# Reordering the opening of a fused cross-attention kernel: form casts and norm statistics later, first loads signalled one by one

## The chip, the cores and the metric

One Trainium2 chip, one core of it. The metric is the device time of one execution in microseconds (us). The engines are TensorE (PE; PEld is its weight load), VectorE (DVE), ScalarE (ACT), GpSimd (POOL) and SyncE (SP), which issues nearly all DMA transfers. Everything is float32; the large products are made of three passes over a rounded part and a remainder of each operand.

## The reference, cut to what matters

First a small attention without softmax over each of 8 batch entries, then two cross-attentions with layer norms and an MLP. Shapes: `x` and the context are (8, 256, 512).

```python
# layer 0, per batch entry b (x_2 is the context)
g_x     = (g_w @ x_2 + g_b).T          # (512, 128)
theta_x = (theta_w @ x + theta_b).T    # (512, 128)
phi_x   = phi_w @ x_2 + phi_b          # (128, 512)
y  = ((theta_x @ phi_x) / 512 @ g_x).T
x  = bn_gamma * (w_w @ y + w_b - bn_mean) * rsqrt(bn_var + eps) + bn_beta + x
# layer 1, seen as (4, 512) tokens a tile group; kv_in is the context both times
h  = layer_norm(x)
x  = x + softmax((h @ wq + bq) @ (ctx @ wk + bk).T / sqrt(128)) @ (ctx @ wv + bv) @ wo + bo   # twice
x  = x + gelu(layer_norm(x) @ w_fc1 + b_fc1) @ w_fc2 + b_fc2
```

## The kernel before, in words

The kernel has a front and a main part. The front computes all keys and values from the context and stores them in DRAM (`kd`, `vd`); the main part walks over heads and token chunks. The change touches the front alone.

The front goes twice over half of the batch: `p` = 0 (batch entries 0 to 3) and `p` = 1 (entries 4 to 7). Each half starts with an **opening** and goes on with eight **rounds** (`r` = 0 to 7, then 8 to 15). `front_order()` writes the order of all units of work out by hand; TensorE, ScalarE and VectorE each walk the same list and do their share of each unit, so the list is the program order of all three. GpSimd and SP have loops of their own.

The opening of a half, in the list written by `opening(p)`, has these units:

- `pg` (two per entry, L1029): the context times the weights of phi and g. VectorE adds the bias and writes `pg` (L1341).
- `M` (L1036): phi and g are multiplied to a 128x128 matrix. ScalarE copies it to `msb` (L1085).
- `th` (L1033): theta from `x`, needs the transfer of `xb`. ScalarE adds the bias and writes `th` (L1083).
- `WM` (L1038): `msb` times the output weights. ScalarE copies it to `wm` (L1087).
- `wy` (two, L1040): `wm` times `th`. ScalarE scales and shifts into `aff` (L1096), VectorE adds `xb` and writes a tile of `x` (L1346). In the kernel before VectorE then takes this tile's statistics for the first layer norm (`tile_stats`, L1312), and after each fourth tile their aggregate and one small addition (`moments`, L1318 and L1320).
- `B` (four blocks `B11, B12, B22, B21` for each of `i` = 0, 1): the context is transposed into a bank of `U` (L876). ScalarE writes the rounded part (`plain`, L1104) and a copy of B12 (`us`, L1108); VectorE writes the remainders (L1362) and four sums and differences, the **forms** T1 to T4 (`temp`, L1371, L1375, L1380, L1385). ScalarE casts each form (`tform`, L1111), and GpSimd makes the form's remainder (`forms_lo`, L647). The forms and their remainders are first needed by the round's products (L842 to L844).

The units `pg`, `M`, `th`, `WM` and `wy` take turns on four PSUM banks (`S` twice, `T`, `O`, by `l0_bank`), so each waits for the reading of the fourth unit before it. The `B` blocks and the units of the rounds take turns on the four banks of `U` (`take`); the second four `B` blocks therefore wait until VectorE is done with the first four.

After the `wy` units of the second entry of a half, ScalarE casts the seven forms of the first key weights (`key_cast`, L1122); GpSimd makes their remainders (`key_form`, L668). A round has 14 key products (`K`, about 1.36 us each on TensorE), and then 14 value products (`V`, in two quarters `q` of seven). VectorE sums these up (`products`, `values`). For the next round VectorE makes three sums of value weights (`value_sums`, L1436, L1439, L1441), in round 0 and 8 right after the opening.

SP issues the loads in its own order: the first context chunk (four loads into `x` that share the semaphore `ctx_in_c[0]`), the weights `wpg` and the bias `pgb_s` (both on `l0_w`), the next chunk, `wth` and `www_s`, `xb` for entry 0, key weights and so on. Each context tile lies in `x`, which is later overwritten by the result. `load_x(b)` for `b` > 1 waits for the counter `z_x` (tiles of `x` written), and behind `load_x(2)` stand the context chunks 2 and 3 and the first value weights.

The wait with which the first product begins, and the place of the form casts in ScalarE's program, are:

```python
pe.wait_ge(ctx_in_c[b // 2], 64)
if name == ("pg", 0, 0):
    pe.wait_ge(l0_w, 32)
...
for form in {B11: (), B12: (T1,), B22: (T3, T2), B21: (T4,)}[blk]:
    act.wait_ge(formed, base + FORMED_BY[p][form])
    act.activation(tform[p][:, 0, form, i, :], temp(i, form), ACT.Copy).then_inc(t_hi, 1)
```

Of the kernel before, what the change touches and what calls it, by code (L numbers as in the profile page):

```python
# [38 lines left out]
P = 128  # L39
# [46 lines left out]


B11, B12, B22, B21 = range(4)
T1, T2, T3, T4 = range(4)
# [40 lines left out]
def opening(p):  # L130

    def blocks(i):
        return [("B", p, i, blk) for blk in range(4)]

    b = 4 * p
    out = [("pg", b, 0), ("pg", b, 1)] + blocks(0)
    for b in range(4 * p, 4 * p + 4):
        more = b + 1 < 4 * p + 4
        out += [("M", b, 0)] + ([("pg", b + 1, 0)] if more else [])
        out += [("th", b, 0), ("WM", b, 0)] + ([("pg", b + 1, 1)] if more else [])  # L140
        out += blocks(1) if b == 4 * p else []
        out += [("wy", b, 0), ("wy", b, 1)]
    return out

# [119 lines left out]
def bass_xattn(nc, x_in, ctx_in, thw, thb, pgw, pgb, www, bncol, wa, wk, wv, wb, hcol, vrow,  # L264
               lncol, f1col, orow, out):
    ctx = ExitStack()
    with ctx:
# [100 lines left out]
        ctx_in_c, x_in_b, l0_w = [sem(f"ctx_in_{c}") for c in range(CHUNKS)], [sem(f"x_in_b{i}") for i in range(2)], sem("l0_w")  # L368
        l0_w2 = sem("l0_w2")
        ident_zero, ident_ready = sem("ident_zero"), sem("ident_ready")  # L370
# [99 lines left out]
        def _(sp):  # L470
# [62 lines left out]

            load_chunk(0)
            sp.dma_start(wpg[:], pgw).then_inc(l0_w, 16)
            sp.dma_start(pgb_s[:], pgb.partition_broadcast(P)).then_inc(l0_w, 16)
            load_chunk(1)
# [88 lines left out]
        def _(pool):  # L626
# [146 lines left out]
            for r in range(ROUNDS):  # L773
# [18 lines left out]
                if not end:  # L792
# [4 lines left out]
                    for k in range(5 if r + 1 < ROUNDS - 1 else 0):  # L797
                        value_form(r + 1, k)
                if r == GROUPS:
                    for c in range(CHUNKS):  # L800
                        deviation(0, c)
# [37 lines left out]
        def _(pe):  # L839
# [33 lines left out]
            def turned_context(o, c, ch):  # L873
                pe.wait_ge(ctx_in_c[c], 64)
                for t in range(4):
                    mm = pe.transpose(o[:, t * P:t * P + P], x[:, 4 * c + t, ch * P:ch * P + P], ident[:])  # L876
                return mm
# [125 lines left out]
            def first_attention(what, b, part):  # L1003
                name = (what, b, part)
                if what == "pg":
                    pe.wait_ge(ctx_in_c[b // 2], 64)
                    if name == ("pg", 0, 0):
                        pe.wait_ge(l0_w, 32)
                elif what == "th":
                    pe.wait_ge(l0_w2, 32)  # L1010
                    pe.wait_ge(x_in_b[b % 2], 16 * (b // 2 + 1))
                elif what == "M":
                    pe.wait_ge(z_free_v, l0_taken(("pg", b, 1), TO_V))
                elif what == "WM":
                    pe.wait_ge(z_free_a, l0_taken(("M", b, 0), TO_A))
                elif what == "wy" and part == 0:
                    pe.wait_ge(z_free_a, l0_taken(("WM", b, 0), TO_A))
# [52 lines left out]
        def _(act):  # L1070
# [28 lines left out]
            def blocks(p, i, blk):  # L1099
                base = formed_before(p, i)  # L1100
                act.wait_ge(unit, UNIT["B", p, i, blk] + 1)
# [3 lines left out]
                if blk == B12:  # L1105
                    if p and i == 0:
                        act.wait_ge(summed, sums_before(GROUPS))
                    act.activation(middle(i), bank("B", p, i, blk), ACT.Copy).then_inc(copied, 1)  # L1108
                for form in {B11: (), B12: (T1,), B22: (T3, T2), B21: (T4,)}[blk]:
                    act.wait_ge(formed, base + FORMED_BY[p][form])  # L1110
                    act.activation(tform[p][:, 0, form, i, :], temp(i, form), ACT.Copy).then_inc(t_hi, 1)  # L1111
# [128 lines left out]
            for what, *a in FRONT:  # L1240
# [12 lines left out]
                elif what == "q":  # L1253
                    if a[2] == 1:
                        queries(*a[:2])
                elif what == "L":
                    exponentials(0)
                elif what == "X":
                    divided(0)
                elif what in TO_A:  # L1260
                    first_attention(what, *a)
                    if what == "wy" and a[0] % 4 == 1 and a[1] == 1:
                        for k in range(7):
                            key_cast(GROUPS * (a[0] // 4), 0, k)

# [29 lines left out]
        def _(dve):  # L1295
# [18 lines left out]
            def moments(n, c):  # L1314
# [5 lines left out]
                dve.tensor_scalar(vpe[:, 4 * c:4 * c + 4], mv[:, 4 * c:4 * c + 4, 1], EPS, None, ALU.add).then_inc(ln_eps, 1)  # L1320

            def normalise(n, c, own=range(4)):

# [10 lines left out]
            def first_attention(what, b, part):  # L1334
                name = (what, b, part)
                o = l0_bank(*name)
                if what == "pg":
                    if b == 4 and part == 0:
                        dve.wait_ge(v_form, 7 * GROUPS)
                    dve.wait_ge(z_unit, L0[name] + 1)  # L1340
                    dve.tensor_tensor(pg[:, 2 * part:2 * part + 2, :], o.rearrange("p (a n) -> p a n", a=2),  # L1341
                                      pgb_s[:].unsqueeze(1).to_broadcast([P, 2, 256]), ALU.add).then_inc(z_free_v, 1)
                elif what == "wy":
                    k = 2 * b + part
                    dve.wait_ge(z_free_a, l0_taken(name, TO_A))
                    dve.tensor_tensor(x[:, k, :], aff[:, part, :], xb[:, b % 2, part, :], ALU.add).then_inc(z_x, 1)  # L1346
                    dve.wait_ge(z_x, k + 1)
                    tile_stats(k)
                    if k % 4 == 3:
                        moments(0, b // 2)  # L1350

# [187 lines left out]
            for k, (what, *a) in enumerate(FRONT):  # L1539
# [10 lines left out]
                elif what == "V":  # L1550
                    r, q, product_of = a
                    values(*a)
                    if (r + 1) % GROUPS and r + 1 < ROUNDS - 1 and q == 0 and product_of in (P6, P7, P3):
                        value_sums(r + 1, (P6, P7, P3).index(product_of))
# [130 lines left out]
```

## Time and profile before

| what | us |
|---|---|
| median of 3 runs (2339.66 to 2346.64) | 2343.88 |
| the profiled execution | 2339.65 |
| its span | 2337.8 |
| PE busy in the span | 2281.9 (98%) |
| DVE, ACT, POOL busy | 1411.3, 1165.5, 1250.0 |
| first opening on TensorE | 9.70 to 59.96 |
| second opening on TensorE | 375.51 to 420.60 |

The profiled execution has 1.85 us outside its span. In the rows of the profile "idle before <-releaser" gives how long the engine had been idle before an instruction and what ended this. TensorE's granted clock is given as a share of its full 2.4 GHz; 0.50 is its lower level, 1.2 GHz. A timeline row with xN is N instructions in a row; its second number is from the first one's start to the last one's end, and TensorE's products overlap their neighbours by some 0.15 us, so that differences of starts are better durations.

### The profile page before, as it was taken

How to read it: one execution, taken by the hardware profiler on the slowest of the kernel's cores; microseconds unless marked ns; L12 is line 12 of the kernel's file. 1: busy time of each engine (PE TensorE's matmuls, PEld its weight loads, DVE VectorE, ACT ScalarE, POOL GpSimd, SP SyncE). 2: the span in 40 equal slices, each digit the busy share in tenths (PEclk: the TensorE clock that was granted, in tenths of full speed). 3: DMA queues.
4: the chain of work that ended last, by engine and by line, in shares of the span. 5: the costliest groups of instructions: out<-in, count | busy, mean ns of one | idle time of the engine just before them, and what ended most of it. 6: DMA issues, size and time to landing. Idle time of an engine off the chain costs nothing.

```text
span 2337.8 us, 36326 instructions
## 1 busy us (share of the span) xinstructions
PE 2281.9 (98%) x13192; PEld 1989.4 (85%) x13192; DVE 1411.3 (60%) x2380; ACT 1165.5 (50%) x2967; POOL 1250.0 (53%) x983
## 2 busy tenths in 40 slices
PE   7999998999999999999999989999999998999999
PEld 5899997899997888888888878888888887788887
DVE  4666666666665666666666776666666666534433
ACT  3323232322224766666666767666666666422222
POOL 3877772887757674344443775644435545611110
PEclk9999999999999999999999999999999999999999
DMA  4454543354544222222222212222222220100001
GB/s 170 145 190 163 190 163 118 127 198 156 194 159 137 72 73 73 69 73 73 66 79 65 73 55 64 73 78 64 76 70 80 75 64 19 36 28 28 27 1 72
DMA packets 83439, 218.33 MB, mean 93 GB/s; under 512 B 9536, under 2 KB 12096, under 8 KB 83264
## 3 DMA queue, kind: packets, MB, share of 16 engines
q1 hardware_dynamic: 82544, 215.91, 27.5%
q8 instruction: 108, 1.77, 0.3%
q14 instruction: 67, 0.55, 0.1%
q10 hardware_dynamic: 720, 0.10, 0.0%
HBM read 144.41 MB, written 71.57 MB: 92 GB/s over the span
## 4 chain that ended last, share of the span: by engine, by line
PE 87%; ACT 5%; DVE 4%; POOL 1%; issue 1%; DMA 1%; SPq 0%; DVEq 0%; ACTq 0%
PE U L842 22%; PE U L844 22%; PE U L843 22%; PE T L987 4%; PE O L842 2%; PE S L844 2%; PE O L844 2%; PE O L843 2%; PE S L843 2%; PE S L842 2%; DVE hT L1494 1%; ACT probs L1221 1%; ACT aff L1180 1%; PE S L1029 1%; ACT probs L1213 1%
## 5 line engine op out<-in xcount | busy, mean ns | idle before, releaser
L1513 DVE TENSOR_TENSOR x<-x,U 128x512 f32<-128x512 f32 x384 | 261.1, 683 | 80.8 <-PE U L844 78.5
L1213 ACT ACTIVATE probs<-S,nm 128x257 f32<-128x257 f32 x512 | 238.2, 477 | 35.8 <-DVE nm L1521 35.8
L1521 DVE TENSOR_REDUCE nm<-S 128x2 f32<-128x514 f32 x256 | 177.3, 692 | 123.1 <-PE S L844 119.3
L1231 ACT ACTIVATE PT<-T 128x512 fp32r<-128x512 f32 x256 | 152.6, 596 | 173.4 <-PE T L987 172.4
L1221 ACT ACTIVATE probs<-probs,rs 128x256 f32<-128x256 f32 x512 | 230.0, 499 | 0.5 <-DVE rs L1525 0.5
L842 PE MATMUL U<-wos,oT 128*128 128x512 f32 x512 | 213.5, 417 | 0.2 <-DVE gT L1504 0.2
L1536 DVE SCALAR_TENSOR_TENSOR oT<-O,hc,oT 128x256 fp32r<-128x256 f32 x256 | 123.8, 484 | 144.0 <-ACT oT L1237 144.0
L739 POOL CAST vb<-vb 128x1024 fp32r<-128x1024 f32 x64 | 68.0, 1063 | 262.4 <-DMA vb<-vd 262.4
L844 PE MATMUL U<-wos,oT 128*128 128x512 f32 x512 | 202.0, 395 | 0.0
L843 PE MATMUL U<-wos,oT 128*128 128x512 f32 x512 | 201.2, 393 | 0.0
L1529 DVE TENSOR_TENSOR PT<-T,PT 128x512 fp32r<-128x512 f32 x256 | 175.5, 686 | 42.0 <-ACT PT L1231 42.0
L1237 ACT ACTIVATE oT<-O,hc 128x256 fp32r<-128x256 f32 x256 | 121.3, 474 | 126.7 <-PE O L844 126.7
L987 PE MATMUL T<-ident,probs 128*128 128x128 f32 x1024 | 154.8, 273 | 14.4 <-ACT probs L1221 14.2
L1199 ACT ACTIVATE tmp<-U,f1c 128x512 f32<-128x512 f32 x64 | 44.0, 688 | 246.1 <-PE U L844 246.1
L733 POOL TENSOR_TENSOR kb<-kb 128x1032 fp32r<-128x1032 f32 x64 | 156.1, 2439 | 5.2
L1504 DVE TENSOR_TENSOR gT<-tmp,gT 128x512 fp32r<-128x512 f32 x64 | 57.2, 893 | 165.8 <-ACT gT L1207 165.8
L842 PE MATMUL U<-hT,wqs 128*128 128x512 f32 x384 | 155.6, 405 | 1.0 <-DVE hT L1494 1.0
L741 POOL TENSOR_TENSOR vb<-vb 128x1024 fp32r<-128x1024 f32 x64 | 153.7, 2402 | 5.1
L842 PE MATMUL S<-kb,qT 128*128 128x258 f32 x512 | 146.5, 286 | 7.2 <-ACT probs L1213 7.2
L844 PE MATMUL U<-hT,wqs 128*128 128x512 f32 x384 | 150.7, 392 | 0.0
L843 PE MATMUL U<-hT,wqs 128*128 128x512 f32 x384 | 150.0, 391 | 0.0
L844 PE MATMUL S<-kb,qT 128*128 128x258 f32 x512 | 145.1, 283 | 0.0
(246 smaller groups left out, 7242.3 us busy)
## 6 DMA issues: line engine op xcount, KB each, us to landing
kd<-stage SPq DMA_DIRECT2D x128, 258.0 KB, 2.5
kb<-kd SPq DMA_DIRECT2D x64, 516.0 KB, 3.4
vd<-stage SPq DMA_DIRECT2D x128, 256.0 KB, 2.1
vb<-vd SPq DMA_DIRECT2D x64, 512.0 KB, 3.8
raw<-wk SPq DMA_DIRECT2D x32, 512.0 KB, 5.3
rawv<-wv SPq DMA_DIRECT2D x28, 512.0 KB, 4.5
raw<-wa SPq DMA_DIRECT2D x24, 512.0 KB, 4.6
raw<-wb SPq DMA_DIRECT2D x24, 512.0 KB, 5.0
```

Of the source, the lines that this page charges most:

```text
L733: pool.tensor_tensor(lo_part_of, f(lo_part_of), f(hi_part_of), ALU.subtract).then_inc(k_lo, 1)
L741: pool.tensor_tensor(lo_part_of, f(lo_part_of), f(hi_part_of), ALU.subtract).then_inc(v_lo, 1)
L842: pe.matmul(o, lhs[0], rhs[0], start=start, stop=False)
L843: pe.matmul(o, lhs[0], rhs[1], start=False, stop=False)
L844: return pe.matmul(o, lhs[1], rhs[0], start=False, stop=stop)
L987: mm = pe.transpose(T[:, at_:at_ + P], probs[:, J % 2, qt, tt * P:tt * P + P], ident[:])
L1213: ins = act.activation(probs[:, r, qt, 0:257], S[:, qt, 0:257], ACT.Exp, bias=nm[:, r, qt:qt + 1], scale=-1.0, accum_out=sums[:, r, qt:qt ...
L1221: ins = act.activation(probs[:, r, qt, 0:256], probs[:, r, qt, 0:256], ACT.Copy, scale=rs[:, r, qt:qt + 1])
L1231: act.activation(PT[:, J % 2, 0, :], T[:], ACT.Copy).then_inc(pt_hi, 1)
L1513: dve.tensor_tensor(x[:, tile, :], x[:, tile, :], bank(what, s, t), ALU.add).then_inc(free, 1)
L1521: dve.tensor_reduce(nm[:, J % 2, :], S[:, :, 0:257], AX.X, ALU.min).then_inc(least, 1)
L1529: dve.tensor_tensor(PT[:, J % 2, 1, :], T[:], f(PT[:, J % 2, 0, :]), ALU.subtract).then_inc(pt, 1)
```

## The change

- In `opening`, the order of the units is another. For the first entry: `M`, `th`, the second four `B` blocks, `WM`, `pg` of the next entry, the two `wy`, the next entry's second `pg`. For the other entries `th` now stands in front of `pg` of the next entry.
- ScalarE's casts of the forms (L1111) leave `blocks` and stand in new units `t`: one behind all units of the half's first entry, one behind those of the second, there with the seven key casts behind it, which keep their place.
- VectorE's `tile_stats` and `moments` leave the opening. Eight tiles' statistics of a half are taken beside the first eight value products of the half's second round (rounds 1 and 9). GpSimd's four `deviation` operations go from the end of its round 8 to that of round 10.
- SP loads `wpg` first; the first context chunk comes as two loads of two tiles each, with a semaphore each (`ctx_first`, `ctx_in_c[0]`); the bias `pgb_s` follows with its own semaphore (`l0_b`), for which VectorE waits in place of TensorE.

```diff
 def opening(p):
-    b = 4 * p
-    out = [("pg", b, 0), ("pg", b, 1)] + blocks(0)
-    for b in range(4 * p, 4 * p + 4):
-        more = b + 1 < 4 * p + 4
-        out += [("M", b, 0)] + ([("pg", b + 1, 0)] if more else [])
-        out += [("th", b, 0), ("WM", b, 0)] + ([("pg", b + 1, 1)] if more else [])
-        out += blocks(1) if b == 4 * p else []
+    first = 4 * p
+    out = [("pg", first, 0), ("pg", first, 1)] + blocks(0)
+    for b in range(first, first + 4):
+        early, more = b == first, b + 1 < first + 4
+        out += [("M", b, 0), ("th", b, 0)]
+        out += blocks(1) if early else [("pg", b + 1, 0)] if more else []
+        out += [("WM", b, 0)]
+        out += [("pg", b + 1, 0)] if early else [("pg", b + 1, 1)] if more else []
         out += [("wy", b, 0), ("wy", b, 1)]
+        out += [("pg", b + 1, 1)] if early else []
+        out += [("t", p, b - first)] if b < first + 2 else []
     return out
...
-            load_chunk(0)
             sp.dma_start(wpg[:], pgw).then_inc(l0_w, 16)
-            sp.dma_start(pgb_s[:], pgb.partition_broadcast(P)).then_inc(l0_w, 16)
+            for i, arrived in enumerate((ctx_first, ctx_in_c[0])):
+                sp.dma_start(x[:, 2 * i:2 * i + 2, :], ctx_in[0, 2 * i:2 * i + 2].rearrange("t p n -> p t n")).then_inc(arrived, 16)
+            sp.dma_start(pgb_s[:], pgb.partition_broadcast(P)).then_inc(l0_b, 16)
             load_chunk(1)
...
-                if r == GROUPS:
+                if r == GROUPS + 2:
                     for c in range(CHUNKS):
                         deviation(0, c)
...
 # scalar engine
-                for form in {B11: (), B12: (T1,), B22: (T3, T2), B21: (T4,)}[blk]:
-                    act.wait_ge(formed, base + FORMED_BY[p][form])
+            def forms(p, i):
+                for form in T_ORDER:
+                    act.wait_ge(formed, formed_before(p, i) + FORMED_BY[p][form])
                     act.activation(tform[p][:, 0, form, i, :], temp(i, form), ACT.Copy).then_inc(t_hi, 1)
...
-                    if what == "wy" and a[0] % 4 == 1 and a[1] == 1:
-                        for k in range(7):
-                            key_cast(GROUPS * (a[0] // 4), 0, k)
+                elif what == "t":
+                    forms(*a)
+                    for k in range(7 if a[1] else 0):
+                        key_cast(GROUPS * a[0], 0, k)
...
 # vector engine
+            def first_norm(p, n):
+                if n < TILES // 2:
+                    dve.wait_ge(z_x, TILES // 2 * (p + 1))
+                    tile_stats(TILES // 2 * p + n)
+                    if n % 4 == 3:
+                        moments(0, 2 * p + n // 4)
...
-                    dve.wait_ge(z_x, k + 1)
-                    tile_stats(k)
-                    if k % 4 == 3:
-                        moments(0, b // 2)
...
                     values(*a)
+                    if r % GROUPS == 1:
+                        first_norm(r // GROUPS, 7 * q + product_of)
```

TensorE's waits follow the loads: entry 0 and the first-chunk blocks wait for `ctx_first`, entry 1 and the blocks for `ctx_in_c[0]` too, and the first product for `wpg` alone.

## Rows read from the trace of the kernel before

**Rows 1.** Waits of TensorE over the span: us in total, times, longest us.
```profile
PE S L1029 <- DMA pgb_s<-pgb: 9.7, 1, 9.7
...
PE S L1038 <- ACT msb L1085: 5.7, 2, 3.0
PE O L1033 <- ACT aff L1096: 5.6, 2, 3.3
PE U L842 <- DVE us L1412: 2.3, 2, 1.1
PE S L1033 <- issue: 1.5, 1, 1.5
...
PE U L842 <- POOL wks L668: 0.4, 2, 0.2
```

**Rows 2.** Timeline of TensorE, first opening: start us, us, instructions, idle before.
```profile
9.70 6.22 PE L1029 MATMUL S<-wpg,x 128*128 128x256 f32 x16 [9.70 <-DMA pgb_s<-pgb]
15.76 1.91 PE L876 MATMUL U<-ident,x 128*128 128x128 f32 x16
...
44.80 1.05 PE L1036 MATMUL S<-pg 128*128 128x128 f32 x8
45.69 1.89 PE L1029 MATMUL S<-wpg,x 128*128 128x256 f32 x8
47.42 1.88 PE L1033 MATMUL T<-xb,wth 128*128 128x512 f32 x4
49.13 0.59 PE L1038 MATMUL O<-www_s,msb 128*128 128x256 f32 x2
...
53.01 1.05 PE L1036 MATMUL O<-pg 128*128 128x128 f32 x8
```

**Rows 3.** Windows: stretch, length, busy us (instructions) by engine, granted clock, DMA share, GB/s.
```profile
22.00:25.00 3.00, 0.01 (x1) 0.00 (x0) 2.36 (x5) 2.19 (x6) 2.63 (x3) 1.00 0.00 0
25.00:28.40 3.40, 3.39 (x8) 2.73 (x9) 0.33 (x1) 0.92 (x2) 1.14 (x1) 0.51 0.00 0
...
35.30:37.40 2.10, 0.00 (x0) 0.00 (x0) 1.34 (x3) 1.40 (x3) 2.08 (x3) 1.00 0.00 0
...
388.00:394.60 6.60, 6.60 (x39) 5.33 (x40) 2.35 (x5) 3.55 (x7) 1.70 (x2) 1.00 0.00 0
```

**Rows 4.** Timeline of ScalarE, first opening.
```profile
24.16 0.63 ACT L1111 ACTIVATE tform<-temp 128x512 fp32r<-128x512 f32 x1 [0.81 <-DVE temp L1385]
...
45.68 0.41 ACT L1122 ACTIVATE wks<-raw 128x256 fp32r<-128x256 f32 x1
...
47.82 0.26 ACT L1085 ACTIVATE msb<-S 128x128 f32<-128x128 f32 x1
```

**Rows 5.** Timeline of VectorE, first opening and the start of round 0.
```profile
18.97 0.69 DVE L1371 TENSOR_TENSOR temp<-us,U 128x512 f32<-128x512 f32 x1 [2.33 <-ACT us L1108]
...
24.05 0.68 DVE L1362 TENSOR_TENSOR plain<-U,plain 128x512 fp32r<-128x512 f32 x1
24.65 0.68 DVE L1341 TENSOR_TENSOR pg<-O,pgb_s 128x512 f32<-128x512 f32 x1
...
63.75 1.15 DVE L1436 TENSOR_TENSOR v_s<-early_v 128x512 f32<-128x512 f32 x1
```

**Rows 6.** Timeline of GpSimd, start of round 0.
```profile
63.60 0.75 POOL L668 TENSOR_TENSOR wks<-raw,wks 128x256 fp32r<-128x256 f32 x1 [8.95 <-ACT wks L1122]
```

**Rows 7.** Timeline of VectorE, value products of round 1.
```profile
126.71 0.69 DVE L1478 TENSOR_TENSOR vt<-vt,U 128x512 f32<-128x512 f32 x1 [0.75 <-PE U L844]
...
132.84 0.69 DVE L1470 TENSOR_TENSOR vt<-U,vb 128x512 f32<-128x512 f32 x1
```

**Rows 8.** DMA issues from 0.7 to 0.75 and from 3.0 to 3.1 us: size, us to landing.
```profile
x<-ctx_in SPq DMA_DIRECT2D x1, 256.0 KB, 3.5
...
wpg<-pgw SPq DMA_DIRECT2D x1, 256.0 KB, 5.1
pgb_s<-pgb SPq DMA_DIRECT2D x1, 128.0 KB, 6.5
```

More of the change, by code:

```diff
@@ L368, in bass_xattn @@
         ctx_in_c, x_in_b, l0_w = [sem(f"ctx_in_{c}") for c in range(CHUNKS)], [sem(f"x_in_b{i}") for i in range(2)], sem("l0_w")
-        l0_w2 = sem("l0_w2")
+        l0_w2, l0_b, ctx_first = sem("l0_w2"), sem("l0_b"), sem("ctx_first")
         ident_zero, ident_ready = sem("ident_zero"), sem("ident_ready")
@@ L873, in turned_context @@
             def turned_context(o, c, ch):
-                pe.wait_ge(ctx_in_c[c], 64)
+                if c == 0:
+                    pe.wait_ge(ctx_first, 16)
+                pe.wait_ge(ctx_in_c[c], 64 if c else 16)
                 for t in range(4):
@@ L1005, in first_attention @@
                 if what == "pg":
-                    pe.wait_ge(ctx_in_c[b // 2], 64)
+                    if b < 2:
+                        pe.wait_ge(ctx_first, 16)
+                    if b:
+                        pe.wait_ge(ctx_in_c[b // 2], 64 if b > 1 else 16)
                     if name == ("pg", 0, 0):
-                        pe.wait_ge(l0_w, 32)
+                        pe.wait_ge(l0_w, 16)
                 elif what == "th":
@@ L1099, in blocks @@
             def blocks(p, i, blk):
-                base = formed_before(p, i)
                 act.wait_ge(unit, UNIT["B", p, i, blk] + 1)
@@ L1339, in first_attention @@
                         dve.wait_ge(v_form, 7 * GROUPS)
+                    if b == 0 and part == 0:
+                        dve.wait_ge(l0_b, 16)
                     dve.wait_ge(z_unit, L0[name] + 1)
```

## The prediction

> **What bounds the kernel now.** I read the page first: TensorE is busy for 98% of the span, so only its idle or slow time can be won. Then its waits, over the whole span [rows 1]: the longest is the 9.7 us before its first product, put down to `pgb_s`, and four more lie in the two openings: `WM` on `msb` (3.0 and 2.7), the second entry's `th` on `aff` (3.3 and 2.2), `th` of entry 3 on what the profile calls issue (1.5, its `xb` transfer), and in rounds 0 and 8 the sixth product on VectorE's `us` (1.1 and 1.2), with 0.4 on GpSimd's key remainders. The rest of the waits lie in the main part, which the change leaves alone. Third, the windows on either side of the stalls, for the granted clock [rows 3]: a stall of 3.0 us (22 to 25) is followed by 3.4 us at 0.51, the lower level (1.2 GHz); one of 2.1 us (35.3 to 37.4) is followed by the same, at 38.8 to 42.1, and the 3.3 us stall of the second opening too, at 400.6 to 403.9; the 2.7 us stall is not (1.00 behind it). (Of these three falls the first has its rows; the others look the same.) So three of four stalls cost 3.4/2 = 1.7 us of slow products on top. Last the timelines of the other engines, for why these waits exist.
>
> **Why they exist.** In the first four `B` blocks VectorE and ScalarE hand work to each other: ScalarE's cast of a form waits for VectorE (0.81 idle, [rows 4]), and the next block's `plain` stands behind that cast, for which VectorE's next form waits. `msb` and `th` stand behind all of it. VectorE takes from 18.97 to 24.65 for seven operations [rows 5], each 0.60 from start to start (24.05 to 24.65), so 4.2 us of work in 5.7. The second four blocks do the same to `aff`, on which the bank of the next `th` hangs.
>
> **The change, part by part.** All times come from differences of starts of the undisturbed third entry [rows 2]: `M` 0.89, a `pg` 1.73, `th` 1.71, then `WM`, `pg` and two `wy` together 3.88 (0.43 + 1.73 + 1.72); an entry is 8.2. Four `B` blocks take 1.74 (15.76 to 17.50), 0.44 each.
>
> *First loads.* TensorE began at 9.70 because `l0_w` counted `pgb_s` too, which landed at 3.05 + 6.5 = 9.55 [rows 8]. The first load of 256 KB landed at 0.72 + 3.5 = 4.2, `wpg`, the fifth, at 2.58 + 5.1 = 7.7: 0.88 us for each 256 KB. The new first product needs 768 KB, so 4.2 + 2 x 0.88 = 5.9. Bounds: 4.9 and 7.7. I take 5.8 to 5.9: **3.9 us**. `pgb_s` lands a little before its old 9.55, and VectorE needs it 3.8 us behind the start, 9.7; at 0.5 us late it would still cost nothing, since `M` wants the sum only at 13.8. Chunk 1 and `xb` are needed 3.8 us earlier but land only some 0.7 earlier; by their old landings (about 12.5 and 14.4) against 12.5 and 14.7 they are just in time, at most 0.3 lost. The first sixteen products take 6.22 us [rows 2] where the second opening's take 3.46: TensorE starts slow, and how long it does may differ by a us from run to run; I leave that out of the sum and in the range. The Trainium skill ("DMA: Bandwidth & Descriptors", Anatomy of one DMA) puts a transfer on GpSimd's path at some 2.0 us plus bytes at 436 GB/s, by which 512 KB issued at 1.2 would be in at 4.4 and the sum 1.4 larger. The trace is slower already for the first 256 KB (3.5 against 2.6), so rows decide.
>
> *Casts of the forms (8 per opening) and the second `B` blocks, first opening.* Shifted by the start, ScalarE's `us` of B12 is there at 15.1, as 18.9 was (the 3.8 includes the one table load). VectorE now runs its 14 form and remainder operations without a gap, at 0.60 from 15.2 to 23.7. TensorE: `pg` to 12.1, blocks to 13.8, `M` 14.7, `th` 16.4. The second blocks need the first's banks, free at 16.6, 17.2, 18.4 and 19.6 (VectorE's 2nd, 3rd, 5th and 7th operation), so the stalls are 0.2 + 0.2 + 0.75 + 0.75 = **1.9** instead of the 3.0 at `WM`. `WM` 20.1, `pg` 20.5, `wy` 22.2, `pg` to 25.7. VectorE: `pg` 23.7, two additions to `x` 24.3 and 25.0, last `pg` 25.8 to 26.5, so `M` of the second entry waits **0.9**. ScalarE has its four casts (2.1 us, at 0.5 each) from 24.9 on, hidden below this.
>
> *Behind the second entry's `wy`* stand four casts (2.1) and the seven key casts (2.1, 45.68 to 47.82 [rows 4]), and behind them `msb` of entry 2. Last `aff` starts at 35.0, casts 35.7 to 39.8, `msb` 40.1. TensorE has `M` to 35.7, `th` and `pg` until 39.1, so `WM` waits **1.0**, where the key casts alone cost nothing. `th` of entry 3 needs `xb` whose issue waits for the fourth tile of `x`, now 36.7; even at the 8 us that it took, 44.8 against a need of 45.1, so the 1.5 go.
>
> *Sum of the first opening:* start 3.9; old stalls 3.0 + 2.2 + 1.5 = 6.7; slow clock 2 x 1.7 = 3.4; new stalls 1.9 + 0.9 + 1.0 = 3.8. 3.9 + 6.7 + 3.4 - 3.8 = **10.2**.
>
> *Second opening,* the same walk with one remainder more per four blocks: old 2.7 + 3.3 + 1.7 = 7.7; new 0.1 + 0.75 + 0.75 in the blocks, 1.1 at `M` (VectorE has 16 operations), 1.0 at `WM`: 3.7. **4.0**.
>
> *Statistics out of the opening.* Behind the last `x` tile VectorE had one statistic between the additions, one behind, and the moments: value sums start at 63.75 [rows 5], and would at 62.1. ScalarE's and GpSimd's chain of casts and remainders hangs on these sums, and so does the sixth product. 1.65 earlier covers its 1.1 stall and the 0.2 of GpSimd: 2.3 + 0.4 = **2.7** for both rounds. GpSimd now has eight form remainders at 1.27 to make later, by 41.3, then seven key remainders and four sums to 49.5; the products start at 49.8 and the next key remainder is wanted at 52.4. Before, it was idle 8.95 us there [rows 6]; about 3 are left. That cover gone, each us is one of TensorE.
>
> *Statistics into rounds 1 and 9.* In the first quarter of the value products VectorE is idle only 0.75 + 0.72 + 0.15 (the largest is in [rows 7]) from its second product on, and seven statistics (0.61) with moments (0.56) are 4.8 us: it comes to the second quarter's first product at 136.0 in place of 132.84. TensorE has four banks, four products of 1.43 = 5.7 us ahead. Walked through, the banks of products 9, 11 and 13 come 0.1 to 0.2 late: **-0.4** a round, -0.8. Bounds: nothing, and all the moved work, 8 x 0.61 + 2 x 0.56 = 6.0 a round. I take the walk, because the idle time and the lead both stand in the rows. The value sums then come 2.6 late, ScalarE's cast of P6 one; GpSimd had 1.95 idle behind. The four deviations on GpSimd move from one round with slack to another: nothing.
>
> **Sum:** 10.2 + 4.0 + 2.7 - 0.8 = **16.1 us**. The profiled execution took 2339.65 (span 2337.8 and 1.85 around it), so 2323.5. It was the fastest of the runs; from their median, 2343.88, it is 2327.8. I say **2328**.
>
> **Rivals.** (B) *The clock falls in the second blocks.* There TensorE works 1.5 of 3.4 us, in pieces of 0.44, less than in any stretch of before outside the stalls. A stall of 2.1 us brought a fall and one of 2.7 us none [rows 3], so length alone doesn't decide, and it could go either way; a fall costs 1.7, in one or both openings: 2330 to 2331. (C) *The moved statistics cost what they weigh.* If VectorE, three units late, holds the banks by its whole extra work, the rounds lose 12.0 in place of 0.8: 2339. For it: VectorE has nearly no idle there; against: 5.7 us of lead. (D) *Slower.* The same place as B, but the clock stays low: many short stalls in place of two long ones, through both openings. TensorE has some 36 us of work in each; each us at half clock costs 0.5. From 32 us of low clock on the gain is gone, and at 46 the kernel is 0.3% slower; at all of 72 it would be 2364. Against: in 44.8 to 53.01 there are no gaps, and the stalls left there are 1.0 long. The Trainium skill ("TensorE: Matmul & The Clock Gate", A second HAM failure mode: psum-queue depth-cycling) says that a kernel that waits in short gaps for PSUM banks between groups of products swings between both clocks. No stretch of this trace shows it; it is the ground for B and D. (E) *More:* chunks land sooner and the blocks' stalls are smaller: 20 us, 2324.
>
> **How the numbers follow.** The forecast (gain 12 to 19) 0.62, B 0.14, C 0.12, D 0.03, E 0.09. A difference under 0.3% (7 us) is about what a measurement of this kernel can't tell from none. Forecast, B and E are faster, with a fifth of C (a partly paid one, as 8 us): 0.87; the rest of C 0.10 the same; D 0.03 slower. The range goes from E, less the 3 us by which medians of these runs differ, to C: 2320 to 2339.
>
> **What would show it.** After: first product near 5.9, first `K` near 49.8 where 59.96 was; no clock of 0.5 between; waits of 0.75 on `formed` before B22 and B21 of the second four, about 1 before `M` of the second entry (on VectorE's `pg`) and before `WM` of the third (on `msb`); second opening 41.1 long in place of 45.1; no wait on `us` in rounds 0 and 8; VectorE without idle time from the second to the tenth value product of round 1. Wrong it would be by a first product behind 7, a wait on `xb` or chunk 1, GpSimd's key remainders late in rounds 0 and 8, or waits of over 1 us on value sums.

## The result and the profile after

The changed kernel took 2321.6 us (median of 5 runs, 2320.61 to 2323.71) beside 2343.18 (5 runs, 2339.66 to 2346.64): ratio 0.9913, 95% interval 0.9899 to 0.9927. The profiled execution took 2323.62 (span 2321.8), 16.0 us less than that of before; the medians are 21.6 apart. Where the other 5.6 lie is told below: the runs of before differ more among themselves, and the profiled one is the shortest of the five.

TensorE's waits over the span in the changed kernel (us in total, times, longest), beside [rows 1]:

```profile
PE T L994 <- ACT probs L1232: 13.8, 15, 2.9
...
PE S L1039 <- DMA x<-ctx_in: 6.0, 1, 6.0
PE U L883 <- DVE plain L1380: 2.2, 4, 0.5
PE O L1048 <- ACT msb L1095: 1.8, 2, 0.9
PE S L1046 <- DVE pg L1363: 1.7, 2, 0.9
...
PE U L847 <- DVE vt L1491: 1.1, 2, 0.7
...
PE U L847 <- DVE stage L1481: 0.9, 2, 0.5
```

The first product waits 6.0 us, and for `x` in place of `pgb_s`. The long waits on `msb` and `aff` (up to 3.0 and 3.3) are gone; in their place stand waits of 0.5 to 0.9 at the places that the prediction named. Those on `us` and `wks` are gone, and 2.0 us of waits on VectorE's value products (`vt`, `stage`) are new (0.2 before).

TensorE's timeline in the first opening, beside [rows 2]:

```profile
6.00 5.16 PE L1039 MATMUL S<-wpg,x 128*128 128x256 f32 x16 [6.00 <-DMA x<-ctx_in]
...
11.76 1.53 PE L883 MATMUL U<-ident,x 128*128 128x128 f32 x12 [0.17 <-DMA x<-ctx_in]
...
17.34 0.66 PE L883 MATMUL U<-ident,x 128*128 128x128 f32 x4 [0.54 <-DVE plain L1380]
18.54 0.65 PE L883 MATMUL U<-ident,x 128*128 128x128 f32 x4 [0.54 <-DVE plain L1380]
...
25.58 1.16 PE L1046 MATMUL S<-pg 128*128 128x128 f32 x8 [0.78 <-DVE pg L1363]
...
39.31 0.70 PE L1048 MATMUL O<-www_s,msb 128*128 128x256 f32 x2 [0.91 <-ACT msb L1095]
...
48.54 0.79 PE L847 MATMUL U<-plain,wks 128*128 128x512 f32 x1
```

These are, in order, the first product, the wait for context chunk 1, the second blocks' stalls, `M` of the second entry, `WM` of the third and the first key product (48.54; 59.96 before). The granted clock over the opening has no fall; the columns of this window are those of [rows 3]:

```profile
0.00:48.50 48.50, 38.94 (x167) 27.41 (x168) 19.38 (x35) 21.53 (x43) 22.17 (x31) 1.00 0.57 205
```

Five positions in the profiled executions measure the front without the main part: the first product, the first key product, the same two of the second half, and the first transpose of the norm (`Z`), with which the main part begins while the last value products still run. Lengths between them, in us:

| kernel | first product | opening 1 | rounds 0 to 7 | opening 2 | rounds 8 to `Z` | first `Z` at |
|---|---|---|---|---|---|---|
| before | 9.70 | 50.26 | 315.55 | 45.09 | 300.57 | 721.17 |
| changed | 6.00 | 42.54 | 314.66 | 40.86 | 300.36 | 704.42 |
| first loads alone | 6.11 | 49.45 | 315.19 | 46.41 | 301.63 | 718.79 |
| casts alone | 9.96 | 42.28 | 315.20 | 39.45 | 300.80 | 707.69 |
| changed, statistics stay | 5.90 | 44.88 | 315.38 | 44.53 | 300.78 | 711.47 |
| changed, old order | 5.99 | 41.80 | 314.65 | 38.74 | 300.72 | 701.90 |
| changed, casts stay | 5.86 | 51.44 | 314.64 | 50.40 | 300.36 | 722.70 |
| changed, statistics spread | 5.97 | 42.75 | 313.30 | 40.87 | 299.00 | 701.89 |
| changed, statistics twice | 5.92 | 43.23 | 317.74 | 40.86 | 303.96 | 711.71 |
| changed, waits for bias | 9.07 | 43.55 | 313.82 | 40.86 | 301.17 | 708.47 |
| changed, key casts late | 6.06 | 41.37 | 314.95 | 39.68 | 300.63 | 702.69 |
| combined | 5.96 | 41.07 | 313.32 | 37.54 | 299.02 | 696.91 |

Opening 1 varies by a us and more between executions of one program, with the time that its first sixteen products take: 5.16 us in the changed kernel's profile, 6.30 in the second profile of the same kernel, whose opening is 43.69 long. The second opening's sixteen take 3.62. The granted clock stands at 1.00 in both places (6.0 to 10.0), so the profile doesn't say what slows the first ones.

### The profile page after: what moved, and what is told of

Its sections match the earlier page's. It is cut to its first block, busy times and chain, and to the rows that moved or that the text cites. A ratio compares the mean times of both kernels' runs of the same rounds, so it can differ in the third digit from the quotient of the medians.

```text
span 2321.8 us, 36328 instructions
## 1 busy us (share of the span) xinstructions
PE 2278.5 (98%) x13192; PEld 1988.7 (86%) x13192; DVE 1407.3 (61%) x2380; ACT 1164.0 (50%) x2967; POOL 1248.3 (54%) x983
## 4 chain that ended last, share of the span: by engine, by line
PE 71%; ACT 4%; DVE 3%; issue 1%; POOL 1%; ACTq 0%; DVEq 0%
PE U L847 17%; PE U L849 17%; PE U L848 17%; PE T L994 5%; PE O L847 2%; PE O L849 2%; PE O L848 2%; PE S L849 2%; PE S L848 2%; PE S L847 2%; DVE hT L1512 1%; ACT probs L1232 1%; ACT aff L1191 1%; ACT probs L1224 1%; DVE gT L1522 1%
```

## The experiments

**First loads alone** (kernel before plus SP's part and the waits that belong to it):

```diff
-            load_chunk(0)
             sp.dma_start(wpg[:], pgw).then_inc(l0_w, 16)
-            sp.dma_start(pgb_s[:], pgb.partition_broadcast(P)).then_inc(l0_w, 16)
+            for i, arrived in enumerate((ctx_first, ctx_in_c[0])):
+                sp.dma_start(x[:, 2 * i:2 * i + 2, :], ...).then_inc(arrived, 16)
+            sp.dma_start(pgb_s[:], pgb.partition_broadcast(P)).then_inc(l0_b, 16)
```

> The kernel before with the first loads of the change alone (order wpg, two tiles, two tiles, bias; a semaphore each). Theory (the first opening is a chain that starts with the first product): first product at 6.0 as in the changed kernel, first K 3.7 us earlier than before (56.3), all stalls of the old opening kept, so 2343.2 - 3.7 = 2339.5. Rival (the transfers behind it, chunk 1 and xb, are not earlier and hold the next step): first K less than 2 us earlier, time within 1.5 us of before.

2336.77 us (12 runs) beside 2340.31 (23 runs): ratio 0.9982 (0.9973 to 0.9990), 3.5 us less, so the start's gain is there in the time. First product at 6.11, first key product at 55.56: 4.4 earlier where 3.7 were expected. The rest is the stall at `WM`, 2.44 where it was 3.0, and the `xb` wait, 1.1 where it was 1.5. In this profile the first `Z` is only 2.4 earlier: the second opening is 1.3 longer and the stretch behind it 1.1. The 1.3 go with a fall of the clock. TensorE stalls for the same 2.73 us at `WM` in the second opening of both kernels, behind the same work; in the kernel before (first row) nothing followed it, here (second row) the products behind it ran at the lower clock (0.60 over 383.3 to 386.7, 1.00 over 388.0 to 391.4 before):

```profile
387.95 0.70 PE L1038 MATMUL S<-www_s,msb 128*128 128x256 f32 x2 [2.73 <-ACT msb L1085]
...
383.19 1.22 PE L1044 MATMUL S<-www_s,msb 128*128 128x256 f32 x2 [2.73 <-ACT msb L1091]
```

So one and the same stall brings a fall in one execution and none in another.

**The bias waited for again** (changed kernel):

```diff
                     if name == ("pg", 0, 0):
                         pe.wait_ge(l0_w, 16)
+                        pe.wait_ge(l0_b, 16)
```

> The changed kernel, its first loads in the new order, but TensorE waits for the bias pgb_s before its first product, as the kernel before did. Theory (of the 3.7 us at the start, most is the semaphore that no longer counts the bias): first product at 8.9 (2.14 + 6.8), 2.9 us later than 6.0, all else shifted by it. Rival (the order of the loads is what counts): first product before 7.

The first product comes at 9.07, 3.1 later, and the kernel takes 2325.88 (4 runs) where the changed one on the same chip took 2322.68: 3.2 more. Of the 3.7 us, 3.1 were the wait for a bias that TensorE never reads; the rest, 0.6, is left for the order of the loads. The TensorE wait of this kernel:

```profile
9.07 6.16 PE L1040 MATMUL S<-wpg,x 128*128 128x256 f32 x16 [9.07 <-DMA pgb_s<-pgb]
```

**Casts alone** (kernel before; the loop over the forms leaves `blocks`, and units `t` stand behind the first two entries' `wy`; order, statistics and loads as before):

```diff
         out += [("wy", b, 0), ("wy", b, 1)]
+        out += [("t", p, b - 4 * p)] if b < 4 * p + 2 else []
```

> The kernel before with the form casts alone moved to the t units; order, statistics and first loads as before. Theory (the casts are the cause of both kinds of stall in the openings): the waits on msb and on aff (11.3) and the three clock falls behind them (5.1) go, a wait of 0.9 before WM of the third entry comes in each opening (1.8), the waits on us stay: 14.6 us less than the kernel before. Rival (order and statistics are needed with them): less than 8 us gained.

2326.52 (5 runs) beside 2339.68 (9 runs): ratio 0.9941 (0.9928 to 0.9955), 13.2 us less. Opening 1 is 8.0 shorter and opening 2 5.6, 13.6 together. Its waits:

```profile
PE U L843 <- DVE us L1415: 2.5, 2, 1.3
PE S L1034 <- issue: 2.0, 1, 2.0
PE O L1039 <- ACT msb L1086: 1.8, 2, 0.9
...
PE T L1041 <- DVE pg L1344: 1.2, 1, 1.2
```

The waits of up to 3.3 are gone and 0.9 before `WM` of the third entry has come twice, as expected; the wait on `xb` grew by 0.5, as the entries in front of it are faster, and one of 1.2 on VectorE's `pg` is new, at a `wy` of the second opening. These 1.7 are about what is missing to the expected 14.6. The three low stretches of the clock in the openings are gone too. This one edit is most of the change.

**Casts stay** (changed kernel, the loop put back into `blocks`, new order kept):

```diff
+                for form in {B11: (), B12: (T1,), B22: (T3, T2), B21: (T4,)}[blk]:
+                    act.wait_ge(formed, formed_before(p, i) + FORMED_BY[p][form])
+                    act.activation(tform[p][:, 0, form, i, :], temp(i, form), ACT.Copy).then_inc(t_hi, 1)
...
                 elif what == "t":
-                    forms(*a)
                     for k in range(7 if a[1] else 0):
```

> The changed kernel with the form casts back inside the B blocks, the new order kept. Theory (the casts in the chain between ScalarE and VectorE are the cause of the old stalls): VectorE's first seven operations take 5.7 us again instead of 4.2, both for the first and second blocks: second blocks and M of the second entry late by 1.5 more each, 3 us per opening, less the 0.9 before WM of the third entry: 2321.6 + 4.2 = 2326. Rival (the order does it): within 1 us of 2321.6.

2342.04 (12 runs) beside 2340.31: ratio 1.0003 (0.9994 to 1.0012). The whole gain is gone: each opening is 9 us longer (8.9 and 9.5) where 2 were expected. TensorE and, under it, ScalarE in the second opening:

```profile
384.64 0.60 PE L1048 MATMUL S<-www_s,msb 128*128 128x256 f32 x2
385.08 1.89 PE L1039 MATMUL S<-wpg,x 128*128 128x256 f32 x8
393.24 2.08 PE L1050 MATMUL T<-th,wm 128*128 128x512 f32 x2 [6.27 <-ACT wm L1097]
```
```profile
390.36 0.63 ACT L1120 ACTIVATE tform<-temp 128x512 fp32r<-128x512 f32 x1 [0.56 <-DVE temp L1400]
390.89 0.58 ACT L1113 ACTIVATE plain<-U 128x512 fp32r<-128x512 f32 x1
392.28 0.63 ACT L1120 ACTIVATE tform<-temp 128x512 fp32r<-128x512 f32 x1 [0.81 <-DVE temp L1405]
392.82 0.37 ACT L1097 ACTIVATE wm<-S 128x256 f32<-128x256 f32 x1
```

`WM` is done at 385.2, but `wm` stands behind the second blocks on ScalarE, which with the casts among them go at VectorE's pace: 6.27 us of wait (3.67 in the first opening), where my expectation had walked only the stalls ahead of `WM`. The new order puts this chain between two steps that TensorE needs one right after the other. It is only bearable with the casts out of it. Behind that long wait the clock was low for 6.8 us in each opening (0.51 over 392.0 to 399.0), which the expectation had not counted either. In the first opening it fell already among the second blocks as well, behind stalls of 0.69, 0.54 and 1.27 us; TensorE's rows there and the windows ahead of the fall and behind it, and last the window at the same place of the second opening:

```profile
17.27 0.65 PE L883 MATMUL U<-ident,x 128*128 128x128 f32 x4 [0.69 <-DVE temp L1395]
18.46 0.66 PE L883 MATMUL U<-ident,x 128*128 128x128 f32 x4 [0.54 <-DVE plain L1382]
20.39 1.12 PE L883 MATMUL U<-ident,x 128*128 128x128 f32 x4 [1.27 <-DVE plain L1382]
```
```profile
16.50:20.00 3.50, 1.39 (x9) 0.84 (x8) 2.84 (x5) 1.94 (x4) 3.42 (x4) 1.00 0.19 71
...
20.20:23.60 3.40, 3.21 (x10) 2.76 (x11) 1.43 (x3) 2.55 (x7) 2.53 (x3) 0.51 0.00 0
...
384.00:387.40 3.40, 2.82 (x14) 2.21 (x14) 1.00 (x3) 2.55 (x7) 1.27 (x1) 1.00 0.00 0
```

This is rival B's mechanism at its place, in a kernel whose gaps there are longer than the changed one's (0.54 at most). But the second opening has nearly the same three stalls, 0.67, 0.54 and 1.27, and its clock stayed at 1.00: such a pattern can bring a fall and need not.

**Old order** (changed kernel with the order of before, `t` units where they are):

```diff
-        out += [("M", b, 0), ("th", b, 0)]
-        out += blocks(1) if early else [("pg", b + 1, 0)] if more else []
-        out += [("WM", b, 0)]
-        ...
+        out += [("M", b, 0)] + ([("pg", b + 1, 0)] if more else [])
+        out += [("th", b, 0), ("WM", b, 0)] + ([("pg", b + 1, 1)] if more else [])
+        out += blocks(1) if b == 4 * p else []
+        out += [("wy", b, 0), ("wy", b, 1)]
```

> The changed kernel with the old order of the small products (pg of the next entry ahead of th, second B blocks behind the second pg), the t units where they are. Theory: with the casts out of the chain the old order has no stall: the second blocks come 6 us behind the first, when VectorE has freed all banks (stalls of 1.1 per opening go), and pg of the second entry is in time for M (0.8 and 0.9 go); first K at about 46.7, second opening 38.9 long in place of 40.9: 2321.6 - 3.9 = 2317.7. The new order would then be a loss inside the gain. Rival (the new order is what removed the stall at WM or at th): waits of 2 to 3 us on msb or aff come back, 2326 or more.

2318.45 (5 runs) beside 2340.31: ratio 0.9902 (0.9888 to 0.9916). This interval and the changed kernel's overlap, so the runs alone don't rank the two; the fronts do: opening 2 is 38.74 long in place of 40.86 and opening 1 0.7 shorter although its first sixteen products took 0.7 longer. Its waits in the openings:

```profile
PE O L1046 <- ACT msb L1093: 1.8, 2, 0.9
...
PE S L1041 <- issue: 1.1, 1, 1.1
...
PE T L1048 <- DVE pg L1361: 0.5, 1, 0.5
```

The 2.2 in the blocks and the 1.7 at `M` are gone, for 1.1 on `xb` and 0.5 on `pg`. By the first `Z` (701.90 against 704.42) the new order of the small products is a loss of some 2.5 us inside the gain; 3.9 were expected.

**Statistics stay** (changed kernel, `tile_stats` and `moments` back behind each addition to `x`, `first_norm` out):

> The changed kernel with the statistics and moments back in the opening. Theory: the waits in rounds 1 and 9 (2.0 us in all) go, the waits on us in rounds 0 and 8 (2.3) and the 0.4 on GpSimd come back, and M of the second entry waits about 1.1 longer in each opening because two statistics stand ahead of pg on VectorE: 2321.6 - 2.0 + 2.7 + 2.2 = 2324.5. Rival (statistics cost the same wherever they are): 2321.6 within 1 us.

2330.72 (6 runs) beside 2340.31: ratio 0.9953 (0.9939 to 0.9967), some 9 us more than the changed kernel where 3 were expected. VectorE and TensorE in its second opening, and the window behind the stall:

```profile
382.13 0.69 DVE L1368 TENSOR_TENSOR x<-aff,xb 128x512 f32<-128x512 f32 x1
382.85 0.69 DVE L1324 BATCH_NORM_STATS2 stats<-x 128x6 f32<-128x512 f32 x1
383.46 1.20 DVE L1368 TENSOR_TENSOR x<-aff,xb 128x512 f32<-128x512 f32 x1
384.69 0.69 DVE L1324 BATCH_NORM_STATS2 stats<-x 128x6 f32<-128x512 f32 x1
385.31 0.67 DVE L1363 TENSOR_TENSOR pg<-S,pgb_s 128x512 f32<-128x512 f32 x1
```
```profile
386.03 1.16 PE L1046 MATMUL S<-pg 128*128 128x128 f32 x8 [2.88 <-DVE pg L1363]
387.03 3.58 PE L1043 MATMUL T<-xb,wth 128*128 128x512 f32 x4
```
```profile
387.00:390.30 3.30, 3.30 (x6) 1.34 (x5) 0.00 (x0) 0.28 (x1) 1.23 (x2) 0.51 0.26 96
```

The stall before `M` grows by 2.0 (0.92 to 2.88) where 1.1 was expected: two statistics, and an addition that takes 1.20 instead of 0.69 while GpSimd is busy. And then the clock falls, 1.7 more, which the expectation did not have. In the first opening the stall grows by 1.0 (0.78 to 1.76), with no fall behind it. The rest of the 7.0 by which the front is longer (711.47 to 704.42) are the waits on `us` and `wks` that come back (3.0), less those in rounds 1 and 9 (2.0), and 1.3 of a slower start, which is chance. The medians differ by 1 to 2 us more than the fronts; where these lie isn't shown. In the old order (casts alone, with its statistics in the opening) `M` has no such wait, so moving the statistics is worth most in the new order. In the old order it was not tried by itself; by the fronts (19.3 gained with it, 13.5 by the casts and 3.7 by the start) I estimate some 2 us for it there.

**Statistics spread:**

```diff
-                    if r % GROUPS == 1:
-                        first_norm(r // GROUPS, 7 * q + product_of)
+                    if r % GROUPS in (1, 2) and q == 1 and product_of in (P1, P6, P2, P3):
+                        first_norm(r // GROUPS, 4 * (r % GROUPS - 1) + (P1, P6, P2, P3).index(product_of))
```

GpSimd's `deviation` operations go one round later with them.

> The changed kernel with the eight statistics of a half beside the second quarter's value products P1, P6, P2 and P3 of its second and third round, where VectorE has no value sums to make, instead of beside eight products in a row. Theory: the waits on vt and stage in rounds 1 and 9 (2.0 us) go and nothing comes: 2.0 less than the changed kernel. Rival (VectorE's second quarter is as full): waits stay within 0.5 of 2.0.

The waits on `vt` and `stage` are not there any more, and the two stretches of rounds are 1.4 shorter each, first `Z` 2.5 earlier. The time was 2323.14 (5 runs, ratio 0.9926, 0.9914 to 0.9939), no less than the changed kernel's: 2.5 us in the front are below what runs of this kernel tell. Its profile has four stretches at the lower clock in the main part, the changed kernel's three. By the trace the theory holds, by the time it is open.

**Statistics twice** (a second `bn_stats` of each tile into an unused buffer):

> The changed kernel with each of the eight statistics taken twice (the second result unused). By theory the four banks' lead is already used up, so each further us of VectorE work in the first quarter is a us of TensorE: seven more statistics at 0.6 are 4.2 us, less the 0.5 still idle: waits of about 4.7 in place of 1.0 per round, 7 us more in all. Rival (the lead still hides it): under 2 us more.

2330.57 (5 runs), ratio 0.9957 (0.9945 to 0.9970). Its waits on the same two:

```profile
PE U L848 <- DVE stage L1483: 4.2, 5, 1.5
PE U L848 <- DVE vt L1493: 2.9, 2, 1.6
```

7.1 in place of 2.0, and the rounds are 3.1 and 3.6 longer: 6.7 for 16 more statistics (9.6 us of VectorE at 0.6 each). So the lead of four banks is nearly used up in the changed kernel: of more work moved there, some 0.7 of each us (6.7 of 9.6) would be paid by TensorE. This is rival C's mechanism at the price at which it bites.

**Key casts late** (unit `c` with the seven key casts behind `WM` of the third entry):

> The changed kernel with the seven key casts in a unit of their own behind WM of a half's third entry; form casts where they are. Theory: msb no longer stands behind them, the wait of 0.9 before that WM goes in both openings (1.8 us less), and GpSimd, busy with form remainders until then, starts its key remainders within 0.5 us of before. Rival: a wait on wks comes in rounds 0 and 8 and eats it.

The 0.9 before that `WM` are gone in both openings and no wait on `wks` came; opening 2 is 39.68 long (40.86), first `Z` 1.7 earlier. 2321.61 (4 runs) beside 2322.68 for the changed kernel, a difference within the spread of both.

**Combined** (old order, moved casts, new first loads, key casts late, statistics spread, and SP's `load_x(3)` ahead of `load_chunk(3)`), run twice. The `deviation` operations go to the end of round 11 here.

> Moved casts and first loads of the change, old order of the small products, key casts in a unit behind WM of the third entry, statistics spread over two rounds (second quarter's P1, P6, P2 and P3), and load_x(3) issued ahead of context chunk 3. Theory: of the waits of the run with the old order, 0.9 twice (msb), 1.1 (xb) and 2.0 (value products) go: 2318.5 - 4.9 = 2313.6, 8 us under the changed kernel. Rival: the key casts, 2.2 us later, make GpSimd's key remainders late in rounds 0 and 8 and a wait on wks of 1 us or more comes.

> The combined kernel once more, beside the changed one. By the fronts of the profiles (first norm's transposes at 696.9 against 704.4) it should be 7.5 us under the changed kernel; a difference under 3 us would mean that its front gives something back in the main part.

First 2317.01 (4 runs, 2313.91 to 2320.92; 2313.6 were expected) beside 2339.68: ratio 0.9901 (0.9887 to 0.9916). Then 2315.73 (4 runs, 2314.46 to 2322.01) beside 2341.72: 0.9893 (0.9876 to 0.9910), with the changed kernel on the same chip:

> The changed kernel as it is, beside the combined one on the same chip. First K at 48.5, second opening 40.9 long, 0.9913 of before within 0.001.

2322.68 (5 runs, 2321.54 to 2326.80), ratio 0.9920 (0.9905 to 0.9935). So 7.0 us less by the medians, with intervals that still touch; its first `Z` comes at 696.91 and 696.34 against 704.42 and 704.96. What is left of waits in its front:

```profile
PE S L1039 <- DMA x<-ctx_in: 6.0, 1, 6.0
...
PE T L1050 <- ACT wm L1097: 1.2, 2, 0.6
PE S L1043 <- issue: 1.0, 1, 1.0
PE T L1050 <- DVE pg L1364: 0.5, 1, 0.5
```

By its front it is 7.5 to 8.6 us ahead of the changed kernel, and by the medians 7.0. Its own two profiled executions took 2314.00 and 2322.01 with fronts that differ by 0.6: the first has one stretch of 3.4 us at the lower clock, the second has seven, all in the main part. The `xb` wait stayed (1.0, and 0.5 the second time), so `load_x(3)` ahead of the last chunk brought half a us at most. Of the changed kernel's own expectation the first key product missed, at 49.65 where 48.5 was expected, for the slower start (6.30 in place of 5.16).

## Why the prediction was right

The sum was 16.1 us, the profiled executions differ by 16.0, and the medians' difference (21.6) has the sign and roughly the size forecast; 2321.6 lies in the range, 6.4 below the 2328 named. It is nearer to rival E's 2324, of which half came: the chunks did not land soon enough to help (0.2 late), and the blocks' stalls were 0.8 and 0.5 smaller than walked. That 16.0 is so near is in part luck: the front is 16.8 shorter, and the main part had three stretches at the lower clock in the profile after and one in that of before. By its steps:

- *First loads, 3.9.* Right: 3.7 in the profile, and the two runs on it show that it was the semaphore. By the formula that the prediction cited from the Trainium skill ("DMA: Bandwidth & Descriptors", Anatomy of one DMA) the first product would have come at 4.4, 1.6 too early; it is stated for GpSimd's path, these loads go by SP's queue, and the measurement decides. Chunk 1 was 0.17 late, inside the 0.3 allowed.
- *Casts out of the chain.* Right in cause and place, and in size within a us. The stalls before the second blocks came as two of 0.54 in each opening, 1.1 where 1.9 and 1.6 were walked, `M` waited 0.78 and 0.92 (0.9 and 1.1), `WM` of the third entry 0.91 both times (1.0). The wait on `xb` of entry 3 went. First key product 11.4 earlier for 10.2, second opening 4.2 shorter for 4.0. In the first, the new stalls are 1.0 less than walked and the first sixteen products took 5.16 instead of 6.22, which is luck that the prediction had left to chance; 0.2 at the start and 0.2 at chunk 1 go the other way, and some 0.5 more isn't placed.
- *No clock of 0.5 in the openings.* Right (rival B did not come, in none of the kernels with the casts moved and the statistics out of the opening). The Trainium skill's rule ("TensorE: Matmul & The Clock Gate", A second HAM failure mode: psum-queue depth-cycling: short waits for PSUM banks make the clock swing) was weighed for it: with two stalls of 0.54 between the blocks the changed kernel's trace shows no fall, and rival D, which needed falls throughout, did not come. With the casts left in place the first opening agrees with that rule, a fall behind three short stalls for `U` banks, 1.27 the longest, and the second opening, with nearly the same stalls and no fall, doesn't. Rival B was a matter of chance, as the prediction put it.
- *Waits on `us` and `wks`, 2.7.* Right: both gone, and back (2.6 and 0.4) when the statistics stay. The two stretches of rounds are together 1.1 shorter, for 2.7 less 0.8 in the sum.
- *Statistics into rounds 1 and 9, -0.8.* The term that was mis-sized: waits of 2.0 us, 1.5 in the second profile. VectorE came to the eighth product when the walk had it: at 122.44, which is 136.1 on the time of the kernel before (13.65 later there), for 136.0. But two operations on the way, each right ahead of a read that TensorE waits for, got longer beside GpSimd (the last two rows are TensorE's products 11 and 13 and the waits before them):

```profile
119.49 1.28 POOL L678 TENSOR_TENSOR wvs<-rawv,wvs 128x512 fp32r<-128x512 f32 x1 [3.25 <-ACT wvs L1148]
...
119.77 1.54 DVE L1459 TENSOR_TENSOR v_s<-v_s,rawv 128x512 f32<-128x512 f32 x1
...
124.02 0.83 DVE L1332 TENSOR_SCALAR vpe<-mv 128x4 f32<-128x4 f32 x1
...
122.06 0.36 PE L847 MATMUL U<-wvs_b,tform 128*128 128x256 f32 x1 [0.47 <-DVE stage L1481]
...
125.58 0.36 PE L847 MATMUL U<-wvs_b,plain 128*128 128x256 f32 x1 [0.42 <-DVE vt L1491]
```

The windows over both, whose fifth term is GpSimd's busy time:

```profile
119.80:121.30 1.50, 1.50 (x14) 1.50 (x14) 1.50 (x3) 0.00 (x0) 0.97 (x1) 1.00 0.45 175
124.00:124.80 0.80, 0.80 (x9) 0.80 (x9) 0.78 (x2) 0.40 (x1) 0.80 (x2) 1.00 0.00 0
```

The value sum had taken 0.68 at 131.46 before, where GpSimd was busy for 0.00 of 0.7 us, and the small addition 0.26 and 0.17; with GpSimd busy they take 1.54 and 0.83. The Trainium skill ("SBUF — State Buffer", SBUF: two separate sides) has a VectorE operation with two inputs in SBUF and a GpSimd operation that reads SBUF exclude each other for a whole instruction; the value sum agrees with it, for it ended at 121.31, 0.54 after GpSimd's operation at 120.77, and 0.6 is its usual length. Another value sum (`rawv`) took 0.68 here where it had 1.23 before, which is why the walk is right on the eighth product all the same; what it missed is where the long operations stand. At their usual lengths the reads of products 7 and 9 would come 0.9 and 1.5 earlier, and TensorE would not have waited for either; this is reckoned from the rows, no run shows it.

- *Which part does it* was not asked in the prediction, and there the runs correct the picture: the casts alone bring 13.2 and the loads 3.5; the new order loses some 2.5; and moving the statistics is worth 7.0 in the front of the new order (1.3 of it chance), after the 1.5 to 2.0 that they cost in rounds 1 and 9.
- *From the profiled execution to the median.* This is the step that missed, by 6.4: I took the runs of before as shifted copies of the profiled one, and started from the median of three, 2343.88. The 41 runs of this kernel that stand beside the experiments have a median of 2340.3 (2337.95 to 2347.44), so 3.6 of the 6.4 are that three runs happened to be long. From 2340.3 the forecast would be 2324.2; 2321.6 and, on another chip, 2322.68 were measured. By the same 41 the change gains some 18 and not 21.6.

  What is left goes with the granted clock. Of the 23 runs on one chip those at 0.997 took 2337.95 to 2340.27 and those at 0.994 or less 2342.71 to 2347.44; the profiled one had 0.997. The changed kernel's ten have 0.997 to 0.999. The profiles show where the low clock lies, in stretches of 3.4 us, in the openings and in the main part: three and one before (0.997); four and four with the first loads alone (0.994), whose openings have the stalls of before; none and three, then none and two, in the changed kernel. So the change takes away the three or four of the openings. In that one profile at 0.994 three of the four more falls than before lie in the main part, which the change leaves alone; whether the changed kernel has fewer there isn't shown.

## What to carry to other kernels

Where two engines hand small operations to each other, take out of that chain all that nobody waits for: here eight casts an opening, each short, set the pace of both engines and through their buffers that of a third, and moving them brought 13.2 us, of some 19 for the whole change on one chip (four fifths by the fronts, 13.5 of 16.8). Ask of each other edit in such a bundle whether it still pays once the main one is made; here the order that looked like filling a gap placed a chain between two steps that had nothing between them. Deferred work needs a place with idle time of its own: a lead of four buffers took it once, and of what was added then most was passed on. And take the time before from more than three runs: here their median was 3.6 us too long, a fifth of the gain.

## What the runs showed of the hardware

- A stall of 2.1 us was followed by 3.4 us at half the clock, one of 2.7 us was not [rows 3]; the same stall of 2.73 us, in the same place of the same opening, was followed by one in the profile with the first loads alone. No single stall needs to be long: three short ones among the blocks (0.69, 0.54, 1.27) brought a fall with the casts left in place, and nearly the same three in its second opening none. With the statistics left in place a stall before `M` of 1.76 us brought none and one of 2.88 did.
- In the main part of one and the same program (the combined kernel) one profiled execution had one stretch of 3.4 us at the lower clock, another seven; they took 2314.00 and 2322.01 us with fronts that differ by 0.6.
- The same first sixteen products took 5.16 to 6.62 us in the profiles, and 3.62 in the second opening, with the granted clock at 1.00 in both places.
- A VectorE operation with two operands in SBUF took up to 1.5 us beside a busy GpSimd where it takes 0.7 alone; even one on 128x4 elements took 0.83 instead of 0.17.
